# Gate and up of 19 chunks as seven block products, with the weight sums made by GpSimd

## The reference

```python
x = layernorm(x + attention(x, wq, wk, wv, wo))      # 32 query heads, 8 key/value heads of 128, window 128
x = layernorm(x + matmul(fake_quant(x), fake_quant(ctx)))
xf = x / 128
inter = silu(xf @ w_gate.T) * (xf @ w_up.T)          # w_gate, w_up: 2752 x 1024, ternary times one scale
inter_q = trunc(clip(inter * 128, -128, 127)).astype(int8)
down = inter_q @ w_down.T                            # w_down: 1024 x 2752, ternary times one scale
x = layernorm(x + trunc(clip(down * 128, -128, 127)).astype(int8))
```

## Time and profile before

| | |
|---|---|
| median of 3 runs | 1512.32 us (1512.27 to 1515.99) |
| span of the profiled execution | 1512.0 us |
| that execution's own time beside its span | not given; the median is 0.3 us above the span |
| TensorE, VectorE, ScalarE, GpSimd busy | 97%, 62%, 48%, 42% |
| moved | 272.66 MB, mean 180 GB/s |

### The profile page before, as it was taken

One profiled execution on the slowest core, in us unless ns is written; L12 is line 12 of the kernel. 1 busy time (PEld: TensorE's weight loads), 2 busy tenths in 40 slices (PEclk: granted clock), 3 DMA queues, 4 the chain that ended last, 5 costly groups with the idle time before them and its releaser, 6 DMA issues.

```text
span 1512.0 us, 23061 instructions
## 1 busy us (share of the span) xinstructions
PE 1472.5 (97%) x7501; PEld 1206.1 (80%) x7501; DVE 943.9 (62%) x1691; ACT 722.1 (48%) x1440; POOL 628.3 (42%) x566
## 2 busy tenths in 40 slices
PE   8899999999999999999999999999799999999996
PEld 6688888888878888888888888887478888888643
DVE  7644444445566677777877777876744444444597
ACT  5433333333444465666666665654652222222564
POOL 0477777776566454555555555534630000000000
PEclk9999999999999999999999999999999999999998
DMA  6477777777652857666676757660102221222111
GB/s 222 157 277 276 275 274 275 274 275 266 218 194 85 319 194 248 224 238 223 228 247 210 265 184 273 202 223 1 56 1 94 101 103 70 104 76 97 50 42 71
DMA packets 103572, 272.66 MB, mean 180 GB/s; under 512 B 12512, under 2 KB 12896, under 8 KB 103520
## 3 DMA queue, kind: packets, MB, share of 16 engines
q1 hardware_dynamic: 103520, 272.02, 51.5%
HBM read 180.75 MB, written 91.23 MB: 180 GB/s over the span
## 4 chain that ended last, share of the span: by engine, by line
PE 63%; DVE 3%; ACT 2%; DMA 2%; issue 1%; POOL 1%; SPq 0%; ACTq 0%; DVEq 0%
PE ps L1116 10%; PE ps L1115 10%; PE ps L938 7%; PE ps L939 7%; PE ps L940 7%; PE ps L1123 5%; PE ps L889 2%; PE ps L890 2%; PE ps L891 2%; PE ps L920 2%; PE ps L921 2%; PE ps L902 2%; PE ps L919 2%; PE ps L1023 2%; DMA q_raw<-q_rows 1%
## 5 line engine op out<-in xcount | busy, mean ns | idle before, releaser
L1115 PE MATMUL ps<-xt_h,w_h 128*128 128x512 f32 x672 | 262.0, 390 | 0.0
L1116 PE MATMUL ps<-xt_l,w_h 128*128 128x512 f32 x672 | 261.5, 389 | 0.0
L870 PE MATMUL ps<-xo_h,wb_h 128*128 128x512 f32 x644 | 251.4, 390 | 6.6 <-ACT c L1264 3.4
L871 PE MATMUL ps<-xo_l,wb_h 128*128 128x512 f32 x644 | 250.7, 389 | 0.0
L872 PE MATMUL ps<-xo_h,wb_l 128*128 128x512 f32 x644 | 250.6, 389 | 0.0
L938 PE MATMUL ps<-wo_h,o_h 128*128 128x512 f32 x512 | 206.3, 403 | 0.0
L939 PE MATMUL ps<-wo_l,o_h 128*128 128x512 f32 x512 | 199.8, 390 | 0.0
L940 PE MATMUL ps<-wo_h,o_l 128*128 128x512 f32 x512 | 199.6, 390 | 0.0
L1767 POOL TENSOR_TENSOR pm_l<-pt_l,upto 128x512 fp32r<-128x512 f32 x64 | 82.5, 1288 | 251.4 <-DVE pt_l L2006 251.4
L870 PEld LDWEIGHTS ps<-xo_h,wb_h 128*128 128x128 f32 x644 | 120.9, 188 | 34.7 <-issue 6.4
L1115 PEld LDWEIGHTS ps<-xt_h,w_h 128*128 128x128 f32 x672 | 126.2, 188 | 26.4
(11 more groups left out here) (188 smaller groups left out, 3130.4 us busy)
## 6 DMA issues: line engine op xcount, KB each, us to landing
raw<-w_att SPq DMA_DIRECT2D x47, 512.0 KB, 5.4
f_raw<-w_gu SPq DMA_DIRECT2D x44, 512.0 KB, 4.9
w_h<-u_gu SPq DMA_DIRECT2D x43, 512.0 KB, 4.1
u_gu<-f_unit SPq DMA_DIRECT2D x42, 512.0 KB, 4.8
wp_raw<-w_att SPq DMA_DIRECT2D x32, 512.0 KB, 5.8
wo_high<-wp_h SPq DMA_DIRECT2D x32, 512.0 KB, 2.8
wo_low<-wp_l SPq DMA_DIRECT2D x32, 512.0 KB, 4.1
q_rows<-c SPq DMA_DIRECT2D x64, 256.0 KB, 2.8
```

What stands on the lines that cost most here:

```text
L870: pe.matmul(prod_ps[i], wh, chunk(xo_h[i], c), start=(i in OPENS and c == 0), stop=False, skip_group_check=True)
L871: pe.matmul(prod_ps[i], wh, chunk(xo_l[i], c), start=False, stop=False, skip_group_check=True)
L1115: pe.matmul(dst, w, xt_h[:, c, rows], start=(c == 0), stop=False)
L1116: last = pe.matmul(dst, w, xt_l[:, c, rows], start=False, stop=(c == DC - 1))
```

## The change

- **Seven block products.** For chunks 2 to 20 the four blocks (gate and up by two batches) come from seven products G1 to G7 of half the depth: 4 depths by 2 parts, 8 matmuls each. G1, G2 and G4 take blocks of the weights as they are; G6, G7, G5 and G3 take the sums S2, S3, S1 and S4 of four blocks of a chunk.
- **Weight sums.** GpSimd makes the four sums (128x512 each) in `weight_sums`; they are small whole numbers and need no low part. There is one set of buffers `ws`, so S3 of the next chunk waits for G7 of this one, S1 for G5, and S4 for G3, which TensorE makes within the next chunk.
- **Operands.** The columns of the second batch are no longer kept as they are. In the slots of tiles 4 to 7 VectorE makes four combinations of the blocks of x in `mix_columns`, ScalarE their high parts (`mixed_high`), GpSimd their low parts (`mixed_low`).
- **Sums of products.** ScalarE copies G1 (`keep_p1`); VectorE adds in five additions per chunk. Up is now read from SBUF by the product with silu. VectorE's order in a chunk is product, truncation of the same unit, additions, then the same for the other batch.
- **Plain chunks.** Chunks 0 and 1 and the left half of the joined rest are made by products of half depth between the last slots.
- **Rows parked.** The normalised rows are written to DRAM (`x2_rows`) and read back (`rows2`) behind the last down weights, since the block products take their place in SBUF.
- **Down weights in two parts.** Eight chunks are loaded in the loop, one for every two chunks; the other fourteen after G4 of the last chunk.
- The branch by the test of the weights is taken three slots earlier than before (ahead of slot 5), and the branch for general weights keeps its form.

The core of the diff:

```diff
@@ TensorE
-            def unit_products(pair, m, by_batch, parts=(0, 1)):
...
+            def half_product(dst, w, operand, start):
+                xh, xl = operand
+                for c in range(KH):
+                    pe.matmul(dst, w[:, c * P:(c + 1) * P], chunk(xh, c), start=(start and c == 0), stop=False, skip_group_check=True)
+                    last = pe.matmul(dst, w[:, c * P:(c + 1) * P], chunk(xl, c), start=False, stop=(c == KH - 1), skip_group_check=True)
+                return last
+            def chunk_products(n, parity, loads, order):
+                first = isinstance(n, int) and n == G_FIRST
+                for k, m, p in order:
+                    if k == G1:
+                        pe.wait_ge(gq_loaded[p], loads)
+                        pe.wait_ge(u_silu, m * 2 - 2)
+                    if k == G6:
+                        pe.wait_ge(u_product, m * 2 - 2)
+                        pe.wait_ge(ws_made, s_count(m, S2_SLOT))
+                    if k == G3:
+                        pe.wait_ge(up_right, g_count(m))
+                        pe.wait_ge(ws_made, s_count(m, S4_SLOT))
+                    if k == G2:
+                        pe.wait_ge(p1_kept, g_count(m))
+                    if k == G7:
+                        pe.wait_ge(u2_made, g_count(m))
+                        pe.wait_ge(ws_made, s_count(m, S3_SLOT))
+                    if k == G5:
+                        pe.wait_ge(u_product, 4 if first else m * 2 - 1)
+                        pe.wait_ge(ws_made, s_count(m, S1_SLOT))
+                    half_product(g_bank(p, k), g_weight(p, k), g_operand(k), k in (G1, G6, G5, G4)).then_inc(g_done, 1)
+            def chunk_of(n, parity, loads):
+                order = [(G1, n, parity), (G6, n, parity), (G3, n - 1, 1 - parity), (G2, n, parity), (G7, n, parity),
+                         (G5, n, parity), (G4, n, parity)]
@@ the last chunk
+                chunk_products(n, 0, n // 2 * 32 + 32, [(k, n, 0) for k in (G1, G6, G2, G7, G4, G5)] + [(G3, n - 1, 1)])
+                pe.wait_ge(u_silu, left(n - 1) + 1)
+                right_product(0, jw)
+                chunk_products(n, 0, 0, [(G3, n, 0)])
@@ GpSimd
+            def weight_sums(n, parity, loads):
+                g = plain(gq[parity][:, :, :])
+                a11, a12, a21, a22 = g[:, 0, 0:HALF], g[:, 0, HALF:DM], g[:, 1, 0:HALF], g[:, 1, HALF:DM]
+                pool.wait_ge(gq_loaded[parity], loads)
...
+                    pool.wait_ge(g_done, g_at(n - 1, G7))
+                pool.tensor_tensor(ws[:, S3_SLOT, :], a11, a21, ALU.subtract).then_inc(ws_made, 1)
+                pool.wait_ge(ws_made, s_count(n, S3_SLOT))
+                pool.tensor_tensor(ws[:, S2_SLOT, :], a22, plain(ws[:, S3_SLOT, :]), ALU.subtract).then_inc(ws_made, 1)
...
+                    pool.wait_ge(g_done, g_at(n - 1, G5))
+                pool.tensor_tensor(ws[:, S1_SLOT, :], a21, a22, ALU.add).then_inc(ws_made, 1)
...
+                    pool.wait_ge(g_done, g_at(n - 1, G3))
+                pool.tensor_tensor(ws[:, S4_SLOT, :], a12, plain(ws[:, S2_SLOT, :]), ALU.subtract).then_inc(ws_made, 1)
@@ ScalarE
+            def chunk_units(n, parity):
+                unit_size(left(n - 1), 1)
+                keep_p1(n, parity)
+                unit_store(left(n - 1), 1, n - 1, 0)
+                right_silu(n - 1, 1 - parity, right(n - 1), 0)
+                left_silu(n, parity)
+                unit_size(right(n - 1), 0)
+                unit_store(right(n - 1), 0, n - 1, 1)
@@ VectorE
+            def second_sum2(n, parity):
+                dve.wait_ge(g_done, g_at(n, G6))
+                dve.wait_ge(p1_kept, g_count(n))
+                wait(dve, u_silu, right(n) - 3)
+                dve.tensor_tensor(c_u2[:, parity, :], g_bank(parity, G6), c_p1[:, :], ALU.add).then_inc(u2_made, 1)
+            def chunk_units(n, parity):
+                left_up(n - 1, 1 - parity, c_u3)
+                dve.wait_ge(up_left, g_count(n) - 1)
+                unit_product(left(n - 1), 1, c_u3[:, :])
+                unit_truncate(left(n - 1), 1)
+                second_sum2(n, parity)
+                right_gate(n - 1, 1 - parity)
+                dve.wait_ge(up_right, g_count(n) - 1)
+                unit_product(right(n - 1), 0, c_low[:, :])
+                unit_truncate(right(n - 1), 0)
+                third_sum2(n, parity)
+                right_up(n, parity)
+            def mix_columns(t):
...
+                dve.tensor_tensor(mixed[0], x12, raw1, ALU.subtract).then_inc(t_made, 1)
...
+                dve.tensor_tensor(mixed[1], x22, mixed[0], ALU.subtract).then_inc(t_made, 1)
...
+                dve.tensor_tensor(mixed[2], mixed[1], raw1, ALU.subtract).then_inc(t_made, 1)
+                dve.tensor_tensor(mixed[3], raw2, mixed[1], ALU.subtract).then_inc(t_made, 1)
+                dve.tensor_tensor(x22_l[:, :, cols], x22, plain(x22_h[:, :, cols]), ALU.subtract).then_inc(x2_taken, 1)
@@ SyncE
+            def load_next(n, e):
+                sp.wait_ge(g_done, g_at(n - 2, G4))
+                sp.wait_ge(ws_made, s_count(n, S4_SLOT) - 8)
+                load_chunk(n, e)
...
+                load_next(G_LAST, 0)
+                sp.wait_ge(g_done, g_at(G_LAST, G4))
+                for c in range(D_NEAR, FC - 1):
+                    sp.dma_start(d_far[:, c - D_NEAR, :], u_dn[c + 3]).then_inc(ud_late[(c - D_NEAR) // 7], 16)
...
+                for t in range(TILES):
+                    sp.dma_start(rows2[:, t, :], x2_rows[t]).then_inc(x2_back[t // TPB], 16)
```

More of the change, by code:

```diff
@@ new lines, in build @@
+        gq = [place(f"gq{e}", [P, 2, DM], F32R, fast(8 * e)) for e in range(2)]
+        ws = place("ws", [P, 4, SEQ], F32R, fast(16))
+        early = place("early", [P, 4, SEQ], F32, fast(32))
+        c_j = place("c_j", [P, SEQ], F32, fast(40))
+        u_round = place("u_round", [P, HALF], F32, fast(42))
+        jw = place("jw", [P, DM], F32R, fast(44))
+        xb_h = place("xb_h", [P, DC, SEQ], F32R, fast(48))
+        xb_l = place("xb_l", [P, DC, SEQ], F32R, fast(64))
+        x22_h = place("x22_h", [P, KH, SEQ], F32R, fast(80))
@@ L1105, in unit_products @@
-            def unit_products(pair, m, by_batch, parts=(0, 1)):
-                i, b = unit_of(m, by_batch)
-                n = pair * 4 + m
-                pe.wait_ge(u_loaded[i], pair * 32 + 32)
-                wait(pe, u_product, n - 3)
-                rows = slice(b * SEQ, (b + 1) * SEQ)
-                for k in parts:
-                    for c in range(DC):
-                        w = w_h[:, 2 * i + k, c * P:(c + 1) * P]
-                        dst = bank(U_BANK[m] + k)
-                        pe.matmul(dst, w, xt_h[:, c, rows], start=(c == 0), stop=False)
-                        last = pe.matmul(dst, w, xt_l[:, c, rows], start=False, stop=(c == DC - 1))
-                if 1 in parts:
-                    last.then_inc(u_done, 1)
@@ new lines, in _ @@
+                right_product(3, gq[1][:, 1, :])
+                pe.wait_ge(t_low, 11)
+                pe.wait_ge(x2_taken, TPB + 1)
+                chunk_of(2, 0, 64)
+                chunk_of(3, 1, 64)
+                with pe.Fori(2, G_LAST // 2 - 1) as r:
+                    for odd in range(2):
+                        chunk_of(r * 2 + odd, odd, r * 32 + 32)
+                for n in (G_LAST - 2, G_LAST - 1):
+                    chunk_of(n, n % 2, n // 2 * 32 + 32)
+                n = G_LAST
@@ L1684, in _ @@
             with act.Else():
+                for i in range(FIRST_SLOT, TILES + 5):
+                    slot(i)
                 act.wait_ge(wo_done, OUT_BLOCKS)
@@ L2340, in unit_truncate @@
                 then(3, integer_part(sizes, u_round[:, :], sizes))
-                with_sign(sizes, sizes, u_val[:, m % 2, :]).then_inc(u_signed, 1)
-            def unit_pair(pair, first, last):
-                for m in range(4):
-                    unit_product(pair, m, last and m % 2 == 1)
-                    if m > 0 and not (last and m == 2):
-                        unit_truncate(pair, m - 1)
-                    if m == 0 and not first:
-                        unit_truncate(pair - 1, 3)
-                    if last and m == 1:
-                        unit_truncate(pair, 1)
+                with_sign(sizes, sizes, u_val[:, e, :]).then_inc(u_signed, 1)
```

745 lines of the change are left out of this document (530 added, 215 removed).

## The result

The changed kernel takes 1542.44 us (median of 4 runs, 1541.82 to 1543.53) against 1512.3 for the kernel before: 1.0194 times, 95% interval 1.0181 to 1.0208. It is slower by 30 us, 5.4 more than forecast.

What follows compares the result with a forecast made beforehand. TensorE, busy 97% of the span, was taken as the bound; 1512.0 - 34.5 + 0.3 + 1.2 + 5.7 + 1.2 + 45.3 + 5.4 = 1536.6 us of span, forecast 1537 us, range 1496 to 1550.

Steps and rivals of the forecast that it cites:

- Matmuls taken away: Gate and up: 19 chunks take 56 matmuls instead of 64, 34.5 us less; TensorE needs 12.71 us per chunk.
- VectorE's queue and GpSimd's holds: Steady chunks: VectorE's queue of 12.10 us plus 3.62 lost to GpSimd's four sums gives 15.7 us per chunk.
- Rivals B and C: Steady chunks: sums fall into VectorE's gaps, 1482 us, chance 0.15; or half the meetings occur, 1511 us, chance 0.15.
- The hold of the port: Shared SBUF ports: GpSimd's sum holds VectorE off until 1.15 us after its start, 0.14 before its recorded end.
- TensorE's two waits per chunk: Steady chunks: TensorE waits about 0.9 us at G2 for the G1 copy and 2.1 at G7 for the second sum.
- Entry: Up to the first chunks: 0.3 and 1.2 us, then chunk 2 waits 5.7 at G2, a later chunk 1.2.
- rival D: Waits in the chunks: the clock falls too, costing 1 us each beyond the slack, 1554 us; chance 0.08.
- Exit: Last chunk: waits of 2.8, 0.9 and 1.7 us, 5.4 in all; late down weights 0, with 5 us kept.
- Sum: Whole kernel: the terms added to the span of 1512.0 give 1536.6 us, forecast as 1537, 25 us slower.
- The step from span to time: Whole kernel: the median of the runs before the change, 1512.32 us, was taken as 0.3 above the span.
- Rival E: Gate and up: the branch for general weights runs, 96 matmuls per chunk, 1679 us at least; chance 0.02.

Runs made afterwards that it cites:

- run 1: The changed kernel with GpSimd's four sums of chunks 3 to 20 made on 32 of 512 columns; 1491.0 us, 0.9851 of the kernel before.
- run 2: The changed kernel with only the sum S4 of chunks 3 to 20 made on 32 columns; 1526.36 us, 1.0087 of the kernel before.
- run 3: The changed kernel with three waits added in GpSimd's program, releasing the same four whole sums at other moments; 1502.12 us, 0.9924 of the kernel before.
- run 11: The changed kernel with only ScalarE's copy of G1 of chunk 2 moved ahead of the fifth early unit's silu; 1536.25 us, 1.0153 of the kernel before.
- run 9: run 6 with the second part of the down weights issued in three steps, after G6, G7 and G4 of the last chunk; 1484.71 us, 0.9811.
- run 6: Kernel with S1 and S4 on VectorE, S3 and S2 on GpSimd, plus chunk 2's G1 copy ahead of the fifth early unit's silu; 1485.98 us, 0.9825.
- run 5: Kernel with S1 and S4 on VectorE, S3 and S2 on GpSimd, plus far down weights in two large transfers; 1492.83 us, 0.9877.
- run 10: run 6 with the parked rows read back only when all down weights have landed; 1485.47 us, 0.9814 of the kernel before.

## Why the prediction was right, and where it was off

- **Matmuls taken away (34.5).** In run 1, where nothing else binds, a chunk takes 12.69 us against the 12.71 of the prediction. Right.
- **VectorE's queue and GpSimd's holds (15.7 us per chunk).** 15.75. The losses were given as 0.57, 0.97, 0.97 and 1.11 and are 0.53, 0.97, 0.97 and 0.97; S4 falls on the step after the rounding and not on it. That the total agrees to 0.05 us is in part luck: the losses are 3.44 in place of 3.62, and VectorE's queue without them is 12.31 (15.75 less 3.44; 13.32 less 0.99 in run 3 gives 12.33) in place of 12.10. Runs 1 and 2 show that the sums cause it (51 us for all, 16 for one), run 3 that what they meet decides, with the same work. Rivals B and C are out: no sum fell into a gap and all four meet a step, since TensorE's products release three of them just ahead of the first truncation and S4 while the rounding of the second runs.
- **The hold of the port.** S2 starts at 1310.68 in run 3, and the product that it delays ends 0.40 us late at 1312.52, so it got the port 0.75 before, at 1311.77: 1.09 us after S2's start and 0.20 before its recorded end. This agrees with the 1.15 of the early stages within 0.06, and not with a hold for the whole recorded instruction. The Trainium skill ("SBUF — State Buffer", "Who interferes with whom") has the pair of ports held for the whole instruction; that rule, taken with the recorded length, is off by these 0.14 to 0.20 us. GpSimd's recorded lengths are rough, so whether the hold or the record is the shorter stays open. The same section of the Trainium skill says that a VectorE operation with at most one input in SBUF, outside the modes that use two ports, doesn't contend. Run 3's additions agree (0.68 to 0.69 us under S3 and S2). The rounding, whose one input is in SBUF, was held up (1.02 us in place of 0.43); which mode it runs in no run here shows.
- **TensorE's two waits per chunk.** Forecast 0.9 and 2.1; idle 0.46 and 1.66, with the rest of the 3.04 us in restarting. The places were right.
- **Entry.** Chunk 2 starts at 1145.94 (1145.6 forecast, wrong from 1148), waits 5.50 at G2 (5.7). The wait was forecast rightly. The start agrees to 0.3 us in part by luck: up to there the code of all these kernels is the same (but for line numbers), and VectorE's first product of the early units starts at 1131.3 in the change's trace, at 1128.3 in run 11's and at 1133.0 in run 9's. The prediction put the wait down to a debt of VectorE; runs 6 and 11 show that most of it hung on one copy's place in ScalarE's queue (1.10 and 1.11 us are left of the 5.5).
- **The clock (rival D, 0.08).** For the steady chunks D is refuted: after 0.46 and 1.66 us without work the granted clock stays 1.00. But at two places it fell to 0.50, the level of 1.2 GHz: after 5.50 us of wait, where 14 matmuls stood 0.43 us apart in place of 0.227 (2.8 us), and after 2.57 us, where 6 did (1.2 us). I had priced D for all waits alike and left it out of the sum for the two longest. The 2.8 us add in full, since VectorE stands for TensorE in chunk 2 (run 11). The 1.2 us mostly don't: the second sum of the last chunk ends at 1437.29, while at full clock TensorE would have been through with G2 at 1434.60 + 8 x 0.227 = 1436.4 and would have waited at G7 for the 0.9 us that the prediction has there. No such wait is in the trace; the slow matmuls took its place.
- **Exit.** Down starts at 1452.65, where the sum gives 1448.5 (1423.88 + 24.6). The second part of the down weights was put at 0, with 5 us kept: it costs 1.0 us, from 1452.65 + 14 x 0.217 = 1455.7 to 1456.7. The text had said that the exit is wrong if these weights end TensorE's wait; they do, by this 1.0 us, so by its own sign the exit was wrong. The possibility was seen, but the term was mis-sized. The DMA engines are all busy (share 1.04) at 360 GB/s. Run 9 shows that an earlier start of the transfers removes the wait; runs 5 and 10 leave open what part SyncE's issuing and the rows' reading have in it.
- **Sum.** The span (1541.8) exceeds the sum (1536.6) by 5.2 us. Counted in starts of TensorE's matmuls against 0.227 us each, 2.8 of it is the clock at the entry, 0.9 the last chunk (6.3 us lost in place of 5.4), 0.3 the start of chunk 2, 0.3 the steady chunks (46.8 in place of 46.5) and 1.0 the far weights; that is 5.3, to within rounding. The step from span to time was wrong: all runs that list both have their time 1.7 to 1.8 us above their span, not 0.3. For the kernel before, the median and the span of the profile are thus most likely from unlike executions, and from that alone the forecast has an uncertainty of 1.4 us. Rival E is out: the lines that run are those of the branch with units.

## What to carry to other kernels

Before VectorE and GpSimd both get work on SBUF, write down at which moment each of GpSimd's operations is released and what VectorE runs then. Against run 1, where the sums are almost nothing, the same four sums cost 51 us when released by TensorE, 11 when released beside VectorE's additions from PSUM, 1.5 when two of them went into VectorE's own stops for ScalarE, and some 10 when VectorE made all four; the version with two in the stops, with one copy moved and the late weights issued as their room came free, takes 1484.7 us, 0.9811 of the kernel before. And where two engines take turns as the bound, price a wait by following it to the next place where the bounding engine itself stands, as run 11 shows, not by whose wait it is.

## What the runs showed of the hardware

- GpSimd's 128x512 addition holds up a VectorE operation on SBUF for about 0.97 us beyond its own 0.69 when the two alternate, and leaves one with an input in PSUM at 0.68 to 0.69, even with two sums back to back (run 3). A rounding with its one input in SBUF is held up as well (0.96 in the change, 1.02 in run 3, in place of 0.43).
- It works both ways, as far as GpSimd's rough records tell: in the change S1 took 1.73 us in place of 1.29 while VectorE's steps ran.
- The granted clock stayed at 1.00 after waits of 1.66 us and below, and went to 0.50 after 2.57 and 5.50 us; it came back sooner after the shorter one (6 matmuls against 14). When it falls is not fixed by the wait alone: behind the same 2.57 us in runs 2 and 11 the first four or five matmuls still ran at 1.00, and only then the clock was at 0.50.
